# A hybrid attention block: transfers, normalising and weight splits at the begin of retention put in another order

## Chip, cores, metric

One core of one Trainium2 chip runs the whole program as one launch. The metric is the device time of that launch in microseconds, as the median of several runs.

## What is computed

The input X is 2 sequences of 2048 rows by 256 numbers. Two layers of retention and feed-forward (FFN) come first, then a ternary FFN, a window attention and a second ternary FFN. The change touches the begin of both retention layers and the FFN behind each. A layer of the reference, cut to what matters:

```python
for i in range(L):                                  # L = 2 layers, H = 8 heads of 32
    Xn = _layernorm(X, ln1_w[i], ln1_b[i])
    Q, K, V = Xn @ WQ[i], Xn @ WK[i], Xn @ WV[i]    # per head
    Q = Q * cosq + _rotate_every_two(Q) * sinq
    K = K * cosk + _rotate_every_two(K) * sink
    Yh = ((Q @ K.T) * decay_mask) @ V
    Y = _groupnorm(Yh, gn_w[i], gn_b[i])
    Y = (silu(Xn @ WG[i]) * Y) @ WO[i] + X
    Yn = _layernorm(Y, ln2_w[i], ln2_b[i])
    X = silu(Yn @ ffn_w1[i] + ffn_b1[i]) @ ffn_w2[i] + ffn_b2[i] + Y
```

The layers get the layernorm of the input, without weights (the kernel normalises its rows of X in place, and folds this into the first layer's scale, hence the factor 1 + EPS).

## The kernel before

**Tiling.** X stays in SBUF as 32 chunks of 128 rows (`X[:, 32, 256]`). Four chunks are a block (`TB`), and blocks alternate between the two sequences: block 0 is chunks 0 to 3, block 1 is chunks 16 to 19. Every product of fp32 numbers is made as three passes over split operands: a high half on ACT (`high_half`, L79, or the second activation of L1486) and a low half on DVE (`low_half`, L85, or L1277).

**The order of work.** Each engine has its own instruction stream, written out by hand; semaphores connect them. `retention` runs `body(i)` over steps of one chunk: a step is `k` of `U = 8`, and chunk `n = 8 i + k - 8` is projected in it, so that `i = 0` only prepares block 0 and chunk 0 starts at `i = 1, k = 0`. In the step of chunk n PE does, in this order: `project_heads(n)` (Q and K, L1645 into `pj`), `scores(n-1)` (L1712), `project_values(n)` (L1645 into `sc`), in even steps `gate_product` (L1645) and `transposes` of the next block's normalised rows (L1687), in odd steps from step 7 on `out_product` and `transpose_outputs`, then `transpose_heads(n)` (L1697), `chunk_out(n-1)` (L1725 to L1736) and `transpose_back(n-2)`. Between them lie: DVE `rotate` (L1288, L1291: reads `pj`), POOL `rotary_sum` (L1194), PE `transpose_heads`, ACT `heads_out` (L1493). `scores(n)` waits for `heads_out(n)`, for DVE's `values(n)` and for `in_done`, which DVE gives in `next_state(n-1)` (L1317).

**A block's rows** are made ready so: DVE `statistics` (L1263, one per chunk) and `aggregate` (L1271), POOL `scales` (five small operations, L1162 to L1177, the power at L1169 the longest), ACT `normalise` (L1462, four) into `xn`, PE `transposes` in two halves of columns (L1687) into the one bank `tr[1]`, ACT `inputs` (two activations per half, L1486), DVE `input_low` (L1277). ACT's `rows_in_place` (L1470) normalises X itself in layer 0.

**Transfers.** In layer 0, SyncE issues X block by block (L1137; it waits for `wqkv` before the second) and then, when all five low halves of the layer's own weights are done, the FFN's weights (L68). ACT issues, ahead of its first computation, `wqkv`, `ident`, `ln1`, `wg`, `wo` and ten tables: 15 issues (L68). It then loads its function table (L1631). DVE centres the value weights (`centre_values`, L1236 and L1239) ahead of the low halves `own_low(0..2)`, and does `own_low(3..4)` at `k = 4`; ACT's high halves match.

**FFN weights** are split during `i = 1`: one `high_half` on ACT and one `low_half` on DVE in each of the eight steps, at the end of a step.

**FFN, POOL.** `body` at L469 makes the scale of block g (L387, L389) and adds constants to the rows of block g - 1 (`add_constants`: L466, and in the second layer L461 ahead of it), in that order per g; at g = 2 it adds those of block 0 as well. DVE `normalise` (L539) of block 3 waits for scale 3, and PE's transposes (L876) for that.

## Time and profile before

| | |
|---|---|
| median of 3 runs | 1512.28 us (1511.6 to 1513.19) |
| the profiled execution | 1512.02 us, span 1510.2 us |
| mean granted clock of TensorE | 0.989 |
| PE / PEld busy | 1441.6 / 1195.5 us |
| DVE / ACT / POOL busy | 1032.2 / 936.4 / 830.2 us |
| PE by 40 slices, in tenths | 4999999999998999999999999998999999989997 |

The span runs from the first to the last instruction; what lies around it is 1.8 us. A slice is 37.8 us; a 9 is a busy share of 90% or more. In the timelines below a line gives start, length, engine, source line, operation, output and inputs, the count of merged instructions, and in brackets how long the engine had been idle and what ended it.

### The profile page before, as it was taken

What the parts mean: (1) busy time and instruction counts of PE and PEld (TensorE: products, weight loads), DVE (VectorE), ACT (ScalarE), POOL (GpSimd) and SP (SyncE); (2) the same over time, 40 slices, a digit from 0 to 9 for tenths busy, and PEclk for the clock granted to TensorE, in tenths of its full rate; (3) what the DMA queues carried; (4) which work ended last, traced back from release to release, by engine and by line L of the source; (5) the groups of instructions that cost most, each with busy time, mean ns of one, the idle gap of its engine ahead of it and who ended that gap; (6) DMA issues with size and microseconds to landing.
All of it is one profiled execution on the core that took longest, in us unless ns stands there. A gap on an engine that the chain in (4) does not pass through costs nothing. (4 is left out here: it accounts for less than half of the span.)

```text
span 1510.2 us, 36387 instructions
## 1 busy us (share of the span) xinstructions
PE 1441.6 (95%) x13066; PEld 1195.5 (79%) x13066; DVE 1032.2 (68%) x2272; ACT 936.4 (62%) x1760; POOL 830.2 (55%) x915
## 2 busy tenths in 40 slices
PE   4999999999998999999999999998999999989997
PEld 3777777899986788888899988886777777768886
DVE  4777877565546887785655678765777777756774
ACT  5555555565554545545655567775777777757775
POOL 2576676412103666663734357776666666636674
PEclk9999999999999999999999999999999999999999
DMA  7000000100001000000300010000000000000101
GB/s 248 2 2 2 0 2 2 36 1 1 1 1 56 2 2 0 1 2 2 124 29 15 1 40 2 0 1 1 2 1 0 0 0 0 0 2 2 40 31 43
DMA packets 21096, 26.27 MB, mean 17 GB/s; under 512 B 1905, under 2 KB 19057, under 8 KB 20849
## 3 DMA queue, kind: packets, MB, share of 16 engines
q1 hardware_dynamic: 18432, 21.64, 4.4%
q10 hardware_dynamic: 2544, 3.04, 0.6%
q8 instruction: 75, 1.23, 0.3%
q14 instruction: 45, 0.36, 0.1%
HBM read 20.48 MB, written 4.19 MB: 16 GB/s over the span
## 5 line engine op out<-in xcount | busy, mean ns | idle before, releaser
L546 DVE TENSOR_TENSOR ffn_h_lo<-ffn_h,ffn_h_hi 128x512 fp32r<-128x512 f32 x112 | 85.8, 766 | 121.6 <-ACT ffn_h_hi L753 121.6
L752 ACT ACTIVATE ffn_h<-ffn_hp,c_b 128x512 f32<-128x512 f32 x112 | 77.2, 689 | 146.3 <-PE ffn_hp L849 145.8
L546 DVE TENSOR_TENSOR ternary_ffn_h_lo<-ternary_ffn_h,ternary_ffn_h_hi 128x512 fp32r<-128x512 f32 x128 | 110.4, 862 | 77.4 <-ACT ternary_ffn_h_hi L753 77.1
L1194 POOL TENSOR_TENSOR ret_qk<-ret_qk,ret_qk_sin 128x512 f32<-128x512 f32 x64 | 82.6, 1290 | 103.5 <-DVE ret_qk_sin L1291 103.1
L860 PE MATMUL ternary_ffn_yp<-down_ternary,ternary_ffn_h_hi 128*128 128x256 f32 x512 | 132.3, 291 | 0.0
L860 PE MATMUL ffn_yp<-down_hi,ffn_h_hi 128*128 128x256 f32 x448 | 127.4, 284 | 0.0
L860 PE MATMUL ternary_ffn_yp<-down_ternary,ternary_ffn_h_lo 128*128 128x256 f32 x512 | 127.4, 280 | 0.0
L1200 POOL TENSOR_TENSOR ret_rstd<-ret_sums,ret_minus_half 128x16 f32<-128x16 f32 x32 | 103.7, 3239 | 42.9 <-DVE ret_sums L1333 42.9
L860 PE MATMUL ffn_yp<-down_hi,ffn_h_lo 128*128 128x256 f32 x448 | 125.0, 279 | 0.0
L860 PE MATMUL ffn_yp<-down_lo,ffn_h_hi 128*128 128x256 f32 x448 | 124.9, 279 | 0.0
L443 POOL TENSOR_TENSOR ternary_ffn_h_sq<-ternary_ffn_h_sq 128x512 f32<-128x512 f32 x61 | 95.0, 1566 | 42.4 <-ACT ternary_ffn_h_sq L759 38.7
L2089 POOL TENSOR_TENSOR win_rms<-win_rms,win_minus_half 128x20 f32<-128x20 f32 x31 | 115.0, 3710 | 2.6
L2313 ACT ACTIVATE wa_probs_t<-wa_tp 128x512 f32<-128x512 f32 x128 | 76.4, 597 | 63.5 <-PE wa_tp L2490 63.0
L752 ACT ACTIVATE ternary_ffn_h<-ternary_ffn_hp 128x512 f32<-128x512 f32 x128 | 76.4, 597 | 54.6 <-PE ternary_ffn_hp L849 48.0
L849 PE MATMUL ternary_ffn_hp<-xt_hi,up_ternary 128*128 128x512 f32 x256 | 103.3, 404 | 4.3 <-DVEq L729 4.3
L849 PE MATMUL ternary_ffn_hp<-xt_lo,up_ternary 128*128 128x512 f32 x256 | 102.6, 401 | 0.0
L860 PEld LDWEIGHTS ternary_ffn_yp<-down_ternary,ternary_ffn_h_hi 128*128 128x128 f32 x512 | 96.4, 188 | 7.1 <-issue 3.8
L860 PEld LDWEIGHTS ternary_ffn_yp<-down_ternary,ternary_ffn_h_lo 128*128 128x128 f32 x512 | 96.6, 189 | 3.2
L1288 DVE TENSOR_TENSOR ret_qk<-ret_pj,rotary 128x512 f32<-128x512 f32 x64 | 44.2, 691 | 71.9 <-PE ret_pj L1645 71.9
L849 PE MATMUL ffn_hp<-xt_hi,up_hi 128*128 128x512 f32 x224 | 88.9, 397 | 2.4 <-DVEq L729 2.4
L1301 DVE TENSOR_TENSOR ret_probs<-ret_sc,causal 128x1024 f32<-128x1024 f32 x64 | 78.4, 1224 | 16.2 <-issue 11.2
L849 PE MATMUL ffn_hp<-xt_lo,up_hi 128*128 128x512 f32 x224 | 88.8, 397 | 0.0
(315 smaller groups left out, 4724.3 us busy)
## 6 DMA issues: line engine op xcount, KB each, us to landing
X<-in_x SPq DMA_DIRECT2D x8, 512.0 KB, 10.1
staging<-in_w SPq DMA_DIRECT2D x4, 1024.0 KB, 8.5
ffn_x_in<-in_x SPq DMA_DIRECT2D x8, 512.0 KB, 3.8
out<-X SPq DMA_DIRECT2D x7, 512.0 KB, 2.9
rotary<-in_rotary ACTq DMA_DIRECT2D x1, 1024.0 KB, 7.5
staging<-in_w_up SPq DMA_DIRECT2D x1, 1024.0 KB, 4.9
staging<-in_w_down SPq DMA_DIRECT2D x1, 1024.0 KB, 7.5
staging<-in_wqkv ACTq DMA_DIRECT2D x1, 768.0 KB, 6.0
```

The source lines that it names most:

```text
L443: nc.gpsimd.tensor_tensor(h_sq[:, m, :], h_sq[:, m, :], h_sq[:, m + 1, :], ALU.add).then_inc(sq_added, 1)
L546: nc.vector.tensor_tensor(h_lo[:, m % R, :], h[:, m % R, :], h_hi[:, m % R, :].bitcast(F32), ALU.subtract).then_inc(h_ready, 1)
L752: nc.scalar.activation(h[:, m % R, :], hp[m % 2][:, :], fn, bias=bias)
L849: last = nc.tensor.matmul(hp[m % 2][:, :], w[:, j, m * P:(m + 1) * P], x[:, k, j, :], start=(n == 0), stop=(n == len(todo) - 1))
L860: last = nc.tensor.matmul(yp[k][t // 2][:, (t % 2) * D:(t % 2 + 1) * D], x[:, m % R, t * P:(t + 1) * P], w[:, m, :], start=(m == 0 and t % ...
L1194: nc.gpsimd.tensor_tensor(qk[:, r, :, :, :], qk[:, r, :, :, :], qk_sin[:, r, :, :, :], ALU.add).then_inc(qk_done, 1)
L1200: nc.gpsimd.tensor_tensor(rstd[:, :], sums[:, 1, :], minus_half[:, :], ALU.pow).then_inc(rstd_done, 1)
L1288: nc.vector.tensor_tensor(qk[:, r, :, :, :], src, cos, ALU.mult)
L1301: nc.vector.tensor_tensor(pr[:, at % 2, :, :, :], sc[:, :, 0:HT].rearrange("p h (j n) -> p h j n", j=NG), causal[:, :].unsqueeze(1).unsque ...
L2089: nc.gpsimd.tensor_tensor(rms[:, 1, :], rms[:, 0, :], minus_half[:, :], ALU.pow).then_inc(rms_work, 1)
L2313: nc.scalar.activation(pt[:, g, :, :].rearrange("p c n -> p (c n)"), tp[:, :], ACT.Copy).then_inc(pt_done, 1)
```

## The change

SyncE issues everything for layer 0 but `ident` and `ln1`: X's first block as four tiles with a semaphore each, `wqkv`, `wg`, `rotary` and `decay`, X's block 1, `wo` and the other tables, the other blocks of X. ACT issues two transfers, loads its function table from a constant that POOL sets, and waits for `ln1` only at its first `inputs`. The scale of blocks 0 and 1 is cut in two on POOL: `first_scale` (add, power), which alone is needed to normalise, and in layer 0 `scale_in_place` for X itself. DVE normalises blocks 0 and 1 (`first_normalise`). The second transposes of block 0 go to `tr[0]`, and `project_heads(0)` starts on the first half of the columns. Block 1's statistics move into chunk 0's step, its normalising and first transposes into chunk 1's; in both layers. `centre_values` moves behind the low halves of Q and K, the splits of values and gate behind `inputs`, that of `out_w` into chunk 0's step. The FFN weights' splits are made two at a time in the last four steps of `i = 1`. In the FFN, scale 3 is made ahead of `add_constants(1)`. The diff, cut to its core (`...` stands for context or for accounting of semaphores):

```diff
                         if begun and isinstance(g, int) and g == 2:      # ffn, POOL
                             add_constants(0, 0, 0)
+                            scales(3, 1)
...
+        def transposed(b, j):
+            return tr[0] if first is not None and at_start(b) and j == 1 else tr[1]
...
-                for b in range(NB):                                      # retention, SyncE
+                for t in range(TB):
+                    sp.dma_start(X[:, t, :], first["x"][P * t:P * (t + 1), :]).then_inc(tile_loaded[t], 16)
+                prefetch(sp, first["weights"][0:1], qkv_loaded)
+                prefetch(sp, first["weights"][1:2], gate_loaded)
+                prefetch(sp, first["tables"][0:2], rotary_loaded)
+                for b in range(1, NB):
                     at = b // 2 + CPB * (b % 2)
-                    if b == 1:
-                        sp.wait_ge(qkv_loaded, 16)
+                    if b == 2:
+                        prefetch(sp, first["weights"][2:], weights_loaded)
+                        prefetch(sp, first["tables"][2:], tables_loaded)
                     sp.dma_start(X[:, TB * at:TB * (at + 1), :],
...
+            def first_scale(b):                                          # POOL
+                pool.wait_ge(mv_done, b + 1)
+                apart(pool, pool_waited)
+                nc.gpsimd.tensor_scalar(work[:, 0, 0, :], mv[:, b, :, 1], ...).then_inc(eps_added, 1)
+                pool.wait_ge(eps_added, b + 1 if first is None else 2 * b + 1)
+                nc.gpsimd.tensor_tensor(scale[:, b, 0, 0, :], work[:, 0, 0, :], minus_half[:, 0:TB], ALU.pow
+                                        ).then_inc(first_scaled, 1)
+            def scale_in_place(b):    # add, power, product, negation for X itself: four operations
...
                     if k % TB == TB - 1 and fresh(2 * i + k // TB):
-                        scales(2 * i + k // TB, k // TB)
+                        if not at_start(i):
+                            scales(2 * i + k // TB, k // TB)
+                        elif k == TB - 1:
+                            first_scale(0)
+                            scale_in_place(0)
+                    if at_start(n):           # behind rotary_sum(0), ahead of rotary_sum(1)
+                        first_scale(1)
+                        if first is not None:
+                            scale_in_place(1)
...
+            def first_normalise(b):                                      # DVE
+                dve.wait_ge(first_scaled, b + 1)
+                if b == 1:
+                    dve.wait_ge(tp_full, KD)
+                for t in range(TB):
+                    last = nc.vector.tensor_scalar(xn[:, t, :], X[:, CPB * TB * b + t, :], mv[:, b, t, 0:1],
+                                                   scale[:, b, 0, 0, t:t + 1], ALU.subtract, ALU.mult)
+                last.then_inc(xn_done, 1)
...
                     if first is not None and at_start(n):
-                        dve.wait_ge(tables_loaded, 16 * len(first["tables"]))
+                        dve.wait_ge(rotary_loaded, 16 * 2)
...
                     if live(n, NT):
                         values(n, k)
+                    if at_start(n):
+                        for t in range(TB):
+                            statistics(1, 0, 1, t)
+                        aggregate(1, 1)
+                        if first is not None:
+                            own_low(4)
+                    if at_start(n - 1):
+                        first_normalise(1)
...
                         if fresh(2 * i + at):
                             input_low(2 * i + at, k % TB // 2, at)
+                        if first is not None and at_start(i) and k == U - 1:
+                            own_low(2)
+                            own_low(3)
...
                     if live(n - 1, NT):
                         next_state(n - 1, k - 1)
...
                     if at_start(i) and k == TB - 2:
                         if first is not None:
+                            first_normalise(0)
+                            for j in range(2):
+                                own_low(j)
                             centre_values()
-                            for j in range(3):
-                                own_low(j)
...
-                    if isinstance(i, int) and i == 1 and k < len(halves):
-                        dve.wait_ge(hi_done, k + 1)
-                        low_half(nc, halves[k])
+                    if isinstance(i, int) and i == 1 and k >= U // 2:
+                        for j in range(2 * k - U, 2 * k - U + 2):
+                            dve.wait_ge(hi_done, j + 1)
+                            low_half(nc, halves[j])
...
-                        if t == 0 and fresh(b + 1):                      # ACT
+                        if t == 0 and fresh(b + 1) and not at_start(b) and not at_start(b + 1):
                             normalise(b + 1, i, at + 1)
...
+                        if t == 2 and first is not None and at_start(b):
+                            act.wait_ge(scale_done, 2)
+                            rows_in_place(1, i, at + 1)
...
                     if live(n, NT):
                         heads_out(n, k)
+                    if at_start(n - 1):
+                        inputs(1, 0, 1)
...
+                    if first is not None and at_start(n):
+                        act.wait_ge(weights_loaded, 16 * (len(first["weights"]) - 2))
+                        own_high(4)
+                        act.wait_ge(tables_loaded, 16 * (len(first["tables"]) - 2))
...
-                prefetch(act, first["weights"][0:1], qkv_loaded)
                 prefetch(act, first["early"], early_loaded)
-                prefetch(act, first["weights"][1:], weights_loaded)
-                prefetch(act, first["tables"], tables_loaded)
-                act.wait_ge(early_loaded, 16 * len(first["early"]))
-                nc.scalar.activation(table_set[:, :], ident[:, 0:1], ACT.Silu)
+                act.wait_ge(consts_set, 1)
+                nc.scalar.activation(table_set[:, :], minus_half[:, 0:1], ACT.Silu)
...
-                    pe.wait_ge(xt_ready, KD * (b + 1))                   # PE, project_heads
+                    pe.wait_ge(xt_ready, 1 if halved else KD * (b + 1))
...
-                        if fresh(b + 1):
+                        if fresh(b + 1) and not at_start(n):
                             transposes(b + 1, t // 2, 4 * i + (k - AHEAD) // 2 + 2)
...
                         chunk_out(n - 1, k - AHEAD - 1)
+                    if at_start(n - 1):
+                        transposes(1, 0, 2)
```

## Rows read from the trace of the kernel before

**Rows 1.** The page, part 1

```profile
PE 1441.6 (95%) x13066; PEld 1195.5 (79%) x13066; DVE 1032.2 (68%) x2272; ACT 936.4 (62%) x1760; POOL 830.2 (55%) x915
```

**Rows 2.** Waits of PE over the whole run: total us, times, longest

```profile
PE ret_tr L1687 <- ACT xn L1462: 19.2, 8, 15.1
```

**Rows 3.** Timeline, first 22 us: start, us, engine, line, operation, [idle before]

```profile
7.24 1.41 DVE L1263 BATCH_NORM_STATS2 ret_stats<-X 128x6 f32<-128x256 f32 x4 [7.24 <-DMA X<-in_x]
...
8.79 0.38 DVE L1271 BATCH_NORM_AGGREGATE mean_var<-ret_stats 128x2 f32<-128x6 f32 x4
...
9.77 0.77 DVE L1239 SCALAR_TENSOR_TENSOR staging<-ret_v_weight_sums,staging 128x256 f32<-128x256 f32 x2
...
10.87 1.90 DVE L85 TENSOR_TENSOR qkv_lo<-staging,qkv_hi 128x512 fp32r<-128x512 f32 x3 [0.33 <-ACT qkv_hi L79]
...
12.91 2.07 ACT L1462 ACTIVATE xn<-X,ret_scale 128x256 f32<-128x256 f32 x4 [1.03 <-POOL ret_scale L1177]
...
15.13 1.09 PE L1687 MATMUL ret_tr<-c_ident,xn 128*128 128x128 f32 x4 [15.13 <-ACT xn L1462]
...
16.25 0.78 ACT L1486 ACTIVATE xt<-ret_tr,c_ln 128x512 f32<-128x512 f32 x1 [0.23 <-PE ret_tr L1687]
...
20.38 0.69 DVE L1277 TENSOR_TENSOR xt_lo<-xt,xt_hi 128x512 fp32r<-128x512 f32 x1 [0.45 <-ACT xt_hi L1486]
```

**Rows 4.** Windows (columns as part 1's engines, then granted clock, DMA share, GB/s)

```profile
12.00:15.00 3.00, 0.00 (x0) 0.00 (x0) 1.20 (x3) 2.09 (x5) 0.68 (x2) 1.00 1.17 319
...
32.40:39.10 6.70, 5.64 (x45) 4.24 (x46) 3.42 (x8) 1.50 (x3) 1.00 (x1) 0.50 0.01 2
```

**Rows 5.** Line L1137: SyncE's issues of X, ns min/median/max

```profile
L1137 SPq DMA_DIRECT2D X<-in_x x8: 387/1004/2057, 0.7 to 13.9; - x8
```

**Rows 6.** Timeline, first steps of layer 0

```profile
21.22 0.77 PE L1645 MATMUL ret_pj<-qkv_hi,xt_hi 128*128 128x512 f32 x1 [2.35 <-DVE xt_lo L1277]
...
25.67 1.29 POOL L1194 TENSOR_TENSOR ret_qk<-ret_qk,ret_qk_sin 128x512 f32<-128x512 f32 x1 [2.07 <-DVE ret_qk_sin L1291]
...
30.10 0.69 DVE L85 TENSOR_TENSOR up_lo<-staging,up_hi 128x512 fp32r<-128x512 f32 x1 [3.85 <-ACT up_hi L79]
...
33.45 1.11 PE L1697 MATMUL ret_tr<-c_ident,ret_qk 128*128 128x128 f32 x4 [2.72 <-POOL ret_qk L1194]
...
39.58 0.73 PE L1712 MATMUL ret_sc<-ret_qkt 32*128 32x128 f32 x16
```

**Rows 7.** Timeline, begin of layer 1's retention

```profile
454.09 0.50 PE L1645 MATMUL ret_pj<-qkv_hi,xt_hi 128*128 128x512 f32 x1 [2.40 <-DVEq L1451]
...
457.60 1.04 POOL L1169 TENSOR_TENSOR ret_scale<-ret_scale_work,ret_minus_half 128x4 f32<-128x4 f32 x1
...
461.53 0.66 PE L1687 MATMUL ret_tr<-c_ident,xn 128*128 128x128 f32 x4 [2.13 <-ACT xn L1462]
...
471.74 0.73 PE L1712 MATMUL ret_sc<-ret_qkt 32*128 32x128 f32 x16
```

**Rows 8.** Timeline, the two feed-forward stages behind the retentions

```profile
291.78 6.63 POOL L466 TENSOR_TENSOR X<-X,c_b 128x256 f32<-128x256 f32 x8
...
292.23 3.04 DVE L539 TENSOR_SCALAR xn<-X,mean_var,scale 128x256 f32<-128x256 f32 x4
...
721.27 1.38 DVE L539 TENSOR_SCALAR xn<-X,mean_var,scale 128x256 f32<-128x256 f32 x4
...
740.96 3.01 DVE L539 TENSOR_SCALAR xn<-X,mean_var,scale 128x256 f32<-128x256 f32 x4 [2.64 <-POOL scale L389]
...
744.02 0.66 PE L876 MATMUL ffn_tp<-c_ident,xn 128*128 128x128 f32 x4 [2.58 <-DVE xn L539]
```

**Rows 9.** Timeline, step 7 of layer 0

```profile
74.33 0.69 DVE L1288 TENSOR_TENSOR ret_qk<-ret_pj,rotary 128x512 f32<-128x512 f32 x1
...
74.94 0.75 DVE L1291 TENSOR_TENSOR ret_qk_sin<-ret_pj,rotary 128x256 f32<-128x256 f32 x2
...
77.55 0.60 PE L1697 MATMUL ret_tr<-c_ident,ret_qk 128*128 128x128 f32 x4
```

More of the change, by code:

```diff
@@ L473, in body @@
                     if not ternary:
-                        if unmeasured(g):
+                        if unmeasured(g) and not first_after_begun(g):
                             scales(g, k)
@@ L1068, in retention @@
         x_loaded = [sem(f"x_loaded{k}") for k in range(NB)] if first is not None else []
+        tile_loaded = [sem(f"tile_loaded{t}") for t in range(TB)] if first is not None else []
+        rotary_loaded, first_scaled, gate_loaded = sem("rotary_loaded"), sem("first_scaled"), sem("gate_loaded")
         x_done = sem("x_done")
@@ L1260, in statistics @@
                     at_least(dve, mv_done, b)
-                    if first is not None and not last_block(b) and not after_last(b):
-                        x_wait(b, at)
+                if first is not None and not last_block(b) and not after_last(b) and (t == 0 or at_start(b)):
+                    x_wait(b, at, t)
                 nc.vector.bn_stats(stats[:, t, :], rows(i, at, t).rearrange("p o d -> p (o d)")
@@ L1406, in body @@
                     if first is not None and at_start(n):
-                        dve.wait_ge(tables_loaded, 16 * len(first["tables"]))
+                        dve.wait_ge(rotary_loaded, 16 * 2)
                     if live(n, NT):
                         rotate(n, i, k - AHEAD)
+                    if first is not None and at_start(n - 1):
+                        dve.wait_ge(tables_loaded, 16 * (len(first["tables"]) - 2))
                     if live(n - 1, NT):
@@ L1429, in body @@
                         next_state(n - 1, k - 1)
[L1430 removed]
+                    if at_start(i) and k >= TB:
+                        pass
+                    elif fresh(2 * i + k // TB) or (after_last(2 * i + k // TB) and i == N):
                         if k % TB < TB - 1:
@@ L1603, in body @@
                     else:
-                        if fresh(b + 1):
+                        if first is not None and at_start(i) and k == TB + 1:
+                            act.wait_ge(early_loaded, 16 * len(first["early"]))
+                        if fresh(b + 1) and not at_start(n - 1):
                             inputs(b + 1, t // 2, at + 1)
+                        if first is not None and at_start(i) and k == U - 1:
+                            act.wait_ge(v_centred, 1)
+                            own_high(2)
+                            act.wait_ge(gate_loaded, 16)
+                            own_high(3)
                         half = (k - AHEAD - 5) // 2
@@ L1639, in _, with three @@
             xs = (xt_hi, xt_lo)
-            def three(out, x, w):
+            def three(out, x, w, second=None):
                 todo = [(j, a, c_) for j in range(KD) for a, c_ in ((0, 0), (0, 1), (1, 0))]
                 for m, (j, a, c_) in enumerate(todo):
+                    if second is not None and m == len(todo) // KD:
+                        pe.wait_ge(xt_ready, second)
                     last = nc.tensor.matmul(out, x(a, j), w(c_, j), start=(m == 0), stop=(m == len(todo) - 1))
@@ L1654, in project_heads @@
                     pe.wait_ge(own_lo_done, 2)
+                halved = at_start(n) and first is not None
                 if at % TB == 0:
-                    pe.wait_ge(xt_ready, KD * (b + 1))
+                    pe.wait_ge(xt_ready, 1 if halved else KD * (b + 1))
                 at_least(pe, qk_read, n)
-                three(pj[0][:, :], tokens(at), lambda a, j: qkv[a][:, j, 0:2 * D]).then_inc(qk_full, 1)
+                three(pj[0][:, :], tokens(at), lambda a, j: qkv[a][:, j, 0:2 * D], KD if halved else None
+                      ).then_inc(qk_full, 1)
             def project_values(n, at):
@@ L1683, in transposes @@
                     pe.wait_ge(yt_read, m - 4)
-                else:
+                elif not (first is not None and at_start(b)):
                     at_least(pe, xt_read, m)
                 for t in range(TB):
-                    last = nc.tensor.transpose(tr[1][:, t * P:(t + 1) * P], xn[:, t, j * P:(j + 1) * P],
+                    last = nc.tensor.transpose(transposed(b, j)[:, t * P:(t + 1) * P], xn[:, t, j * P:(j + 1) * P],
                                                ident[:, :])
@@ L1763, in out_product @@
                 pe.wait_ge(gy_ready, q + 1)
+                if at_start(q) and first is not None:
+                    pe.wait_ge(own_lo_done, 5)
                 if live(q + 3, 2 * NB):
```

53 lines of the change are left out of this document (31 added, 22 removed).

## The prediction, made before the changed kernel had run

> **What bounds the kernel now.** The page comes first: PE is busy 95% of the span and every other engine less than 70% [rows 1], so a microsecond counts only where PE stands still or runs at a lower clock. The waits of PE say where: 19.2 us on ACT's normalised rows, 15.1 of them at the very begin [rows 2]. I then read the begin as a timeline. X's first block is there at 7.24, DVE measures it until about 9.2, five POOL operations and four ACT operations follow, PE's first transposes stand at 15.13, and project_heads(0) starts at 21.22 [rows 3, 6]. Behind that, rotate(1) sits behind a weight split (DVE idle 3.85 for it), PE idles 2.72 for POOL's sum, and from 32.4 to 39.1 the granted clock is 0.50, that is 1.2 GHz, after PE's pause ahead of 33.45 [rows 4, 6]. scores(1) at 39.58 is my first marker: from there the steps are PE's own work. Layer 1 has the same shape, smaller: start 454.09, a wait of 2.13 for ACT's rows, scores(1) at 471.74 [rows 7]. The second FFN has a wait of PE of 2.58, behind DVE, which waited 2.64 for POOL's scale [rows 8]. So 21.2 + 18.4 us, 17.65 us and 2.6 us are what the change can touch.
>
> **Layer 0, up to project_heads(0).** It removes: the whole block as one transfer, four of the five POOL operations, ACT's normalising, and the wait of the second transposes for tr[1]. Transfers: the earliest block came at 7.24 while wqkv shared the engines. Alone at 319 GB/s or more [rows 4], 512 KB take 1.6 us less 0.4 for the last tile's neighbours; issues cost 0.39 us at least [rows 5]. I put the last tile at 5.0 (between 4.4 and 5.9). wqkv now stands behind X on one queue, but both had landed by 9.8, when DVE used them, and the bytes ahead of it are no more than then, so it is there before DVE is free for it at 9.0. Then: one tile's statistics, 1.41/4 = 0.4, gives 5.4; aggregate with its gap 0.5, so 5.9; add and power on POOL with two hand-overs, 0.6 + 1.04 [rows 7], 7.6; first_normalise(0) 1.38 [rows 8], 9.0; transposes 1.1, 10.1; two activations 1.5, 11.6. DVE meanwhile does own_low(0..1), 2 x 0.63 = 1.3, and centre_values, reduce and two operations, about 1.45 from the 0.77 of the two [rows 3], so it is free at 11.75; input_low 0.69, 12.45. With a hand-over PE starts at 12.6 instead of 21.22: **8.6 us earlier** (bounds 6.4 and 9.3). The second half of the columns is ready at 13.8, under the first three passes. rotary is 2.7 MB down the queue, at 319 GB/s there by 11.8; rotate(0) wants it at about 15.6. values and gate are split by 15.1, in time. ACT's table load disappears beside the transfers: nothing, and 1.3 us are there to cover it.
>
> **Layer 0, to scores(1).** values(0) and gate(0) end at about 18.3 if PE's first 4 us (my assumption) go at the pace of its first pass, 0.77 [rows 6], heads(0) 18.5 to 19.0, project(1) until 20.5. DVE now has block 1's statistics (1.41 + 0.5) behind values(0), so mv stands at 19.25. What is queued behind it matters: POOL does first_scale(1), 0.6 + 1.04 + 0.3, and then scale_in_place(1), four operations, some 2.7 us, *ahead of* rotary_sum(1), 1.29 [rows 6]. That sum ends at about 24.8, though rotate(1) is over at 22.8 (itself 0.9 late behind own_low(4) and block 2's first statistics). PE stands for 2.2 us at heads(1), about what it stands now. Then heads(1) and chunk_out(0), 2.1, give 26.9, the moved transposes 0.6, 27.5. Here the change adds a wait that was not there: DVE's input_low(1, 0) stands ahead of next_state(0), and scores(1) waits for in_done. Transposes 27.5, ACT's two activations 29.0, input_low 29.7, state 30.0: scores(1) at 30.0 instead of 28.6. rotate(2), behind them, is late by 0.4 more. 30.4 - 12.6 = 17.8 against 18.4: **0.6 us less**. The old stretch at 1.2 GHz (6.7 us, PE busy 5.64) goes with its cause, but a pause of 2.2 us ahead of a step is of the size that brought it; I charge 1.2 us for a stretch of half that length. **Net -0.6 + 1.2 = +0.6**; bounds -2.5 (no low clock, no 2.2 us pause in full) and +3.
>
> **Layer 1.** Block 1's statistics no longer stand ahead of rotate(0), and PE's 2.13 us wait and its 0.5 us of transposes leave step 0: heads(0) at 459.4. project(1) 1.5, scores and values 1.5, POOL's sum in step with rotate(1) (there is no scale in place here, and the power ends at 460.9), heads(1) at 464.3; 2.05 and 0.6 bring 466.9; the new chain ACT, input_low, state takes 2.5: 469.4, and rotate(2) 0.35. 469.75 against 471.74: **-2.0 us** (bounds 0 and -3.2, the latter without the chain).
>
> **FFN.** In the first one scale 3 waits for DVE either way; 0. In the second the scale moves ahead of add_constants(1), which occupied POOL for some 7 us (eight such operations take 6.63 in the first FFN): DVE's 2.64 go. DVE's four operations still run beside POOL's additions, 3.0 us, from 738.3 to 741.3, and PE wants them at 741.45: **-2.4 us** of 2.58 (bounds 1.6 and 2.6).
>
> **Weight splits, two per step.** The first four steps lose 0.68 us of DVE each, which PE's waits hide. In step 7 rotate starts at 74.33 without any idle time ahead of it [rows 9]: the extra 0.66 and about 0.2 inherited from step 6 push it by 0.86. Its two operations and POOL's sum need 0.69 + 0.75 + 1.29, ending at 77.05, and PE takes it at 77.55: 0.5 us of cover, so **+0.4 us per layer**, +0.8 (bounds 0 and 1.7). Without that cover it would be 0.86 in each.
>
> **Sum.** -8.6 + 0.6 - 2.0 - 2.4 + 0.8 = -11.6. From the profiled 1512.0 this gives 1500.4; the median shown is 0.3 higher, so I write **1500.5**.
>
> **A rule against this change.** DVE's four normalising operations take 1.38 us with POOL idle and 3.04 beside POOL's additions, which began first [rows 8]. In the new order first_normalise(0) runs beside scale_in_place(0), and first_normalise(1) beside rotary_sum(1). My sum takes 1.38, since the nearer POOL operations have 4 numbers per partition and not 256. The Trainium skill (SBUF — State Buffer, section Who interferes with whom) says that such a DVE operation and a GpSimd operation lock a shared port pair, and that the second to issue is blocked for the whole of the first. By that rule the trace agrees for the large additions, and a power of 1 us would hold DVE as well; it would make the sum 1503.7, as rival 1, where the rows as I read them give 1500.5.
>
> **Rivals.**
> 1. *DVE and POOL block each other.* Price 3.04 - 1.38 = 1.66 in full ahead of project_heads(0), and 1.66 less some 0.8 of cover in front of the moved transposes, in each layer: +3.3, **1503.7**. For it: the rows just named. Against it: small operations. 0.18.
> 2. *PE stays at 2.4 GHz and the tiles come early.* -2.5 instead of +0.6 in layer 0's steps, and 0.6 from the transfer: **1497**. 0.12.
> 3. *The doubled splits become the bound.* DVE has no idle time ahead of rotate(7) now; if every one of the four steps pays 0.66 in both layers, +5.3 - 0.8: **1505**. Against it: two of the four steps have a rotation that waits for PE. 0.04.
> 4. *The new order hides nothing*, because wqkv, now behind X on one queue, lands as late as it is early now: if own_low waits until 20, project_heads(0) starts as before and only 3 us of the rest are left: **1509**, within or next to no change. Against it: the bytes ahead of it are the same as before. 0.03.
> 5. *Slower.* DVE's statistics of block 2 stand in chunk 0's step, ahead of rotate(1), and wait for that block's transfer, now SyncE's 19th issue and 4.5 MB down one queue. At 319 GB/s it is there at about 18, and rotate(1) wants DVE at 21.4. Issues took up to 2.06 us under load [rows 5]; nineteen such, 39 us, would hold every engine for 18 us: **1518**. It decides from a landing at 33 us on. Against it: a median of 1.0, and the queue's total is unchanged. 0.02.
>
> **How the numbers follow.** The forecast has 0.61, the rivals 0.18, 0.12, 0.04, 0.03 and 0.02. The range 1496.5 to 1505 takes in the forecast's bounds as far as they are independent (their squares' sum is about 4 us), and rivals 1 to 3. 0.2% is 3.0 us, about what a measurement of this kernel can tell: faster 0.95, same 0.03, slower 0.02.
>
> **What would show it.** Right: project_heads(0) at 12 to 13.5; first_normalise(0) near 1.4; scores(1) 17 to 19 us later; PE idle some 2 us at heads(1) in layer 0, for POOL; in both layers a short PE wait ahead of scores(1), for DVE's state; scores(1) of layer 1 15.5 us after its start instead of 17.65; no wait of DVE for the FFN's scale; PE's transposes of step 7 released by POOL. Wrong: first_normalise at 3 us (rival 1), a wait of DVE for X in chunk 0's step (5), of ACT for wqkv beyond 9 us (4), or a granted clock of 0.5 over more than one stretch behind project_heads(1).

## The result, and the profile after

The changed kernel takes 1498.1 us in the median of 4 runs (1496.82 to 1500.4), the kernel before 1512.7 (1511.6 to 1513.19, 4 runs): a ratio of 0.9909, 95% interval 0.9898 to 0.9921, 14.6 us less where 11.8 were forecast. The profiled execution took 1497.22 us, 14.8 less than the profiled one of before.

The page of the changed kernel, parts 1 and 2. PE's busy time is 10.4 us less [rows 1] though its instructions are about the same in number: stretches at half the clock have gone, and not only waits.

```profile
PE 1431.2 (96%) x13034; PEld 1188.7 (79%) x13066; DVE 1035.8 (69%) x2284; ACT 929.8 (62%) x1748; POOL 831.9 (56%) x915
...
PEclk9999999999999999999999999999999999999999
```

Waits of PE over the run (total us, times, longest). The 19.2 us for ACT's rows [rows 2] are 9.9 for DVE's, once, and 3.0 for ACT's; the last row, 2.2 us for DVE's state (1.08 in each layer), is new.

```profile
PE ret_tr L1773 <- DVE xn L1406: 9.9, 1, 9.9
PE ret_tr L1783 <- POOL ret_qk L1233: 8.4, 8, 2.1
...
PE ret_tr L1773 <- ACT xn L1536: 3.0, 7, 1.2
...
PE ret_sc L1798 <- DVE ret_state_in L1366: 2.2, 2, 1.1
```

The begin as a timeline (start, us, engine, line, operation, idle before), the counterpart of [rows 3]. The tiles are there one by one, POOL does two operations ahead of DVE's rows and not five, and project_heads(0) starts at 13.53, not 21.22 [rows 6]. DVE's rows take 1.39 though POOL's power runs beside them (8.77 to 9.83).

```profile
5.49 0.77 DVE L1312 BATCH_NORM_STATS2 ret_stats<-X 128x6 f32<-128x256 f32 x2 [1.49 <-DMA X<-in_x]
...
7.33 1.04 POOL L1201 TENSOR_TENSOR ret_scale<-ret_scale_work,ret_minus_half 128x4 f32<-128x4 f32 x1
8.41 1.39 DVE L1406 TENSOR_SCALAR xn<-X,mean_var,ret_scale 128x256 f32<-128x256 f32 x4 [1.62 <-POOL ret_scale L1201]
...
8.77 1.06 POOL L1209 TENSOR_TENSOR ret_scale<-ret_scale_work,ret_minus_half 128x4 f32<-128x4 f32 x1
9.30 1.15 ACT L79 ACTIVATE qkv_hi<-staging 128x512 fp32r<-128x512 f32 x2 [6.13 <-DMA staging<-in_wqkv]
...
12.69 0.69 DVE L1326 TENSOR_TENSOR xt_lo<-xt,xt_hi 128x512 fp32r<-128x512 f32 x1
...
13.53 0.77 PE L1729 MATMUL ret_pj<-qkv_hi,xt_hi 128*128 128x512 f32 x1 [1.65 <-DVE xt_lo L1326]
```

The first steps of layer 0 and the begin of layer 1, timelines of the same execution. heads(1) waits 2.11 for POOL in layer 0; in layer 1, scores(1) waits 1.08 for the state, which stands behind ACT's two activations and input_low. Compare [rows 6, 7].

```profile
25.05 0.66 PE L1783 MATMUL ret_tr<-c_ident,ret_qk 128*128 128x128 f32 x4 [2.11 <-POOL ret_qk L1233]
...
458.50 0.77 ACT L1560 ACTIVATE xt_hi<-ret_tr,c_ln 128x512 fp32r<-128x512 f32 x1
...
459.30 0.69 DVE L1326 TENSOR_TENSOR xt_lo<-xt,xt_hi 128x512 fp32r<-128x512 f32 x1 [2.51 <-ACT xt_hi L1560]
459.91 0.22 DVE L1366 TENSOR_TENSOR ret_state_in<-ret_sc,ret_own_state 128x64 f32<-128x64 f32 x1
...
460.27 0.73 PE L1798 MATMUL ret_sc<-ret_qkt 32*128 32x128 f32 x16 [1.08 <-DVE ret_state_in L1366]
```

Where the 14.9 us of the span come from, by the starts of PE's work in the two profiles:

| | before | after | gained |
|---|---|---|---|
| project_heads(0) | 21.22 | 13.53 | 7.7 |
| from there to scores(1) | 18.36 | 16.73 | 1.6 |
| scores(1) to scores(8) | 49.77 | 50.60 | -0.8 |
| layer 1, start to scores(1) | 17.65 | 14.62 | 3.0 |
| scores(1) to scores(8) | 49.18 | 49.96 | -0.8 |
| second FFN | 168.97 | 166.24 | 2.7 |
| window attention and second ternary FFN, which the change doesn't touch | 475.7 | 474.2 | 1.5 |

The rows agree with the stages to 0.1. The last one is chance: over the twelve other executions profiled in this case the window attention alone took 323.8 to 326.4 us, and in the two profiles compared here these last stages hold four stretches of 3.4 us at a granted clock of 0.5 before, two after, ahead of the one at the very end that both have.

### The profile page after: what moved, and what is told of

Same layout as the page of the kernel before. It is cut to its first block and busy times, and to the rows that moved or that the text cites. A ratio compares the mean times of both kernels' runs of the same rounds, so it can differ in the third digit from the quotient of the medians.

```text
span 1495.3 us, 36363 instructions
## 1 busy us (share of the span) xinstructions
PE 1431.2 (96%) x13034; PEld 1188.7 (79%) x13066; DVE 1035.8 (69%) x2284; ACT 929.8 (62%) x1748; POOL 831.9 (56%) x915
## 3 DMA queue, kind: packets, MB, share of 16 engines
q8 instruction: 75, 1.23, 0.3%
```

## The experiments

Each is an edit of the changed kernel, shown shortened; where a range follows the time it is that of 4 runs. They are judged by starts of PE's instructions, which repeat better than the total: scores(1) to scores(8) in layer 0 was 50.58 to 50.61 in the seven executions that have the changed kernel's steps 1 to 7. The start of layer 1 is that of its project_heads(0); expectations that speak of layer 1's first transposes mean the same point.

**1. The transfers as before.**

```
-  SyncE: X by tiles, wqkv, wg, rotary, X block 1, wo and tables, X ...
+  SyncE: X block 0 in one, wait for wqkv, X blocks 1 to 7
+  ScalarE: wqkv, identity and norm, wg, wo, tables
```

> Undo only the transfers: ScalarE issues wqkv first, then identity, norm, wg, wo and tables; SyncE issues X's first block as one transfer and the rest behind wqkv. Theory (the early tiles are a term of their own): DVE's last first-block statistics end at about 8.7 instead of 5.8, project_heads(0) starts 2.3 to 2.9 us later than 13.53, at 15.8 to 16.4, and the whole is longer by 2.3 to 2.9 us. Rival (wqkv's landing sets the pace, since ScalarE's first weight half waited for it until 9.3 in the changed kernel): wqkv lands earlier here, the chain on it is shorter, and project_heads(0) moves by less than 1 us.

1500.84 us (1498.7 to 1503.13). The first statistics stand at 7.21, where the kernel before had them [rows 3], and project_heads(0) at 15.88:

```profile
7.21 1.41 DVE L1304 BATCH_NORM_STATS2 ret_stats<-X 128x6 f32<-128x256 f32 x4 [7.21 <-DMA X<-in_x]
...
15.88 0.77 PE L1726 MATMUL ret_pj<-qkv_hi,xt_hi 128*128 128x512 f32 x1 [1.64 <-DVE xt_lo L1318]
```

So the transfers' order is worth 2.35 us against the profile, and 3.1 against the median of the begin (below). The edit moves wqkv as well as the tiles, but the tiles alone set the start: from the end of DVE's last first-block statistics (8.61 here, 6.26 in the changed kernel's profile) to project_heads(0) it is 7.26 or 7.27 us in all twelve executions with this chain, wherever between 7.23 and 10.23 ACT began to split wqkv. The rival falls.

**2. Layer 0's first block normalised on ACT, with the whole scale.**

```
-  POOL: first_scale(0), scale_in_place(0);  DVE: first_normalise(0)
+  POOL: scales(0, 0) (both kinds);          ACT: own_high(0..1), normalise(0)
```

> Undo only the way in which layer 0's first block is normalised: the five-operation scale on POOL and four activations on ACT, behind ACT's two weight halves, as before. Theory (a term of its own): POOL's last scale operation ends about 1.9 us after first_scale's power, so at about 10.3, ACT's four rows take about 1.6, the rows are done at about 12, against 9.8, and project_heads(0) starts at about 15.7, 2.2 us later than 13.53. Rival (DVE's own chain of weight halves and value centring sets the start of project_heads(0), since input_low stood behind it): DVE has 1.4 us less to do, and project_heads(0) moves by less than 1 us.

1502.16 us (1500.68 to 1503.37). project_heads(0) at 16.10, 2.57 later (3.4 against the median). Counted from the last statistics, which takes the transfers' spread out, it is 10.11 instead of 7.27, so this part is worth 2.84. DVE's weight splits and value centring were over at 11.14 here and PE still had no rows until 12.51, so they are not what sets the start:

```profile
10.29 2.07 ACT L1536 ACTIVATE xn<-X,ret_scale 128x256 f32<-128x256 f32 x4 [1.36 <-POOL ret_scale L1191]
10.38 0.76 DVE L1287 SCALAR_TENSOR_TENSOR staging<-ret_v_weight_sums,staging 128x256 f32<-128x256 f32 x2
...
12.51 1.94 PE L1774 MATMUL ret_tr<-c_ident,xn 128*128 128x128 f32 x8 [12.51 <-ACT xn L1536]
```

Of the 7.7 us at project_heads(0) in the table, 2.4 are the earlier statistics (8.64 before, 6.26 after) and 5.3 the shorter chain behind them (12.58 before, 7.27 after). Experiment 2 explains 2.84 of the 5.3; the rest (the second half of the columns under the first passes, tr[0], the order on DVE) was not taken apart.

**3. Layer 1's begin as before.**

```
-  moved for both layers: at_start(n)
+  moved for layer 0 alone: first is not None and at_start(n)
```

> Undo only layer 1's begin: block 1's statistics in the steps behind project(0), its five-operation scale, ACT's rows and PE's transposes in step 0, as before. Theory (the removed wait and the two DVE blocks ahead of rotate(0) are worth 2 us): layer 1's scores(1) comes 17.0 to 17.7 us after its first transposes instead of 14.62, its scores(8) 2 to 2.3 us later, and the whole is 2 to 3 us longer. Rival (luck of the granted clock: the kernel before had stretches at 0.5 in layer 1 and the changed one has none): without such a stretch the old order costs less than 1 us.

1501.04 us (1499.18 to 1502.03). Layer 1's scores(1) comes 17.60 us after its start, not 14.62, scores(8) 2.77 later, and the whole is 2.9 to 3.9 longer by the medians of the two sets of the changed kernel. PE's wait for ACT's rows is back, at 3.7 us (2.13 in [rows 7]). The rival spoke of an execution without a low stretch, and this was none: the granted clock is 0.75 over six us. The old begin brought the pause and the low stretch in both executions that have it; they were not told apart, and their sum is the price. The eleven profiles that have the moved begin in layer 1, and no weight split in its first three steps, show no such stretch behind heads(1), so its absence there is not the luck of one execution. First the wait (total, times, longest), then the window (busy time of PE, PEld, DVE, ACT, POOL, granted clock, DMA share, GB/s):

```profile
PE ret_tr L1776 <- ACT xn L1539: 6.7, 8, 3.7
```

The window behind that wait:

```profile
456.00:462.00 6.00, 5.17 (x48) 3.56 (x48) 3.13 (x6) 2.05 (x4) 1.27 (x1) 0.75 0.00 0
```

**4. The FFN's scale behind add_constants.**

```
-  if unmeasured(g) and not first_after_begun(g): scales(g, k)
-  scales(3, 1)                 (it stood behind add_constants(0, 0, 0), which stays)
+  if unmeasured(g): scales(g, k)
```

> Undo only the order of scale 3 and add_constants in the FFNs. Theory: PE's wait of 2.6 us behind DVE's normalising, and DVE's of 2.6 for POOL's scale, are back in the second FFN and only there: from its first PE instruction to that of the first ternary FFN it takes 168.9 us instead of 166.2, the first FFN's 166.9 stays within 0.2, and the whole is 2.6 us longer. Rival (the gain was the clock's): the wait is back, and the second FFN's length changes by less than 1 us.

1502.53 us (1500.74 to 1502.67). DVE waits 2.65 us again, PE's wait for xn is 2.6, the second FFN takes 169.00 and not 166.24, the first stays (166.92, 166.91):

```profile
731.68 1.04 POOL L389 TENSOR_TENSOR scale<-ffn_scale_work,ffn_powers 128x4 f32<-128x4 f32 x1
...
732.75 3.01 DVE L539 TENSOR_SCALAR xn<-X,mean_var,scale 128x256 f32<-128x256 f32 x4 [2.65 <-POOL scale L389]
```

So this part is worth 2.76 us: the stage took 166.2 in all twelve profiled executions that have it, and 169.0 in the two that don't. The whole is 4.4 to 5.3 us longer by the medians, more than the 2.6 expected. In the profiled execution much of the excess lies where the edit doesn't reach: the granted clock is low for 6.8 us in layer 0 (24.4 to 31.2), and layer 1's project(0) has a stretch too, so that its scores(1) comes 15.55 after the start and not 14.61:

```profile
447.60:451.00 3.40, 3.40 (x13) 2.94 (x12) 1.08 (x3) 0.00 (x0) 0.65 (x2) 0.51 0.82 254
```

**5. One weight split per step, as before.**

```
-  if ... i == 1 and k >= U // 2:  for j in (2 * k - U, 2 * k - U + 1)
+  if ... i == 1:                  for j in (k,)
```

> Undo only the spacing of the FFN's weight splits: one in each of the steps 0 to 7, as before, with all else as in the changed kernel. Theory (two splits in step 7 cost 0.4 to 0.6 us in each layer): scores(8) stands 49.8 to 50.0 us behind scores(1) in layer 0 instead of 50.60, and 49.2 to 49.4 in layer 1 instead of 49.96, as it did in the kernel before. Against it, DVE's 0.68 us of split 0 and of split 1 stand ahead of rotate(1) and rotate(2), so that scores(1) comes 0.3 to 0.7 us later in layer 1. Rival (the loss in step 7 belongs to the moved begin, not to the splits): both distances stay at 50.6 and 50.0.

One run, 1510.9 us, beside 1511.43 of the kernel before: nearly the whole gain is gone. This was in neither theory, which had scores(1) of layer 1 later by 0.7 at most: it is 3.9 later, and in layer 0 project_heads(0) to scores(1) takes 28.14 instead of 16.73. The splits did give back what was expected, scores(2) to scores(8) falls from 43.30 to 42.70 in layer 0 and from 42.67 to 42.10 in layer 1; but split 0 in step 0 waits for the FFN's weights, whose transfer starts when out_w is split, and DVE's rotate(1) is behind it:

```profile
21.10 0.89 SPq L68 DMA_DIRECT2D staging<-in_w  x2
...
29.76 0.63 ACT L79 ACTIVATE up_hi<-staging 128x512 fp32r<-128x512 f32 x1 [9.41 <-DMA staging<-in_w]
30.42 0.69 DVE L85 TENSOR_TENSOR up_lo<-staging,up_hi 128x512 fp32r<-128x512 f32 x1 [9.01 <-ACT up_hi L79]
...
33.78 0.47 PE L1783 MATMUL ret_tr<-c_ident,ret_qk 128*128 128x128 f32 x1 [11.61 <-POOL ret_qk L1233]
```

It costs layer 1 as well: ACT's half waits for the landing there, 7.79 us after the start, and rotate(1) follows the low half without a pause.

```profile
463.83 0.63 ACT L79 ACTIVATE up_hi<-staging 128x512 fp32r<-128x512 f32 x1 [1.35 <-DMA staging<-in_w]
```

In the kernel before DVE waited for the same split, where I had not looked: a new row of its trace,

```profile
463.90 0.69 DVE L85 TENSOR_TENSOR up_lo<-staging,up_hi 128x512 fp32r<-128x512 f32 x1 [4.91 <-ACT up_hi L79]
```

But there it was not the landing that ended last. ACT began its half at 463.25, right behind heads_out(0), which had waited for PE and so for the rows; and rotate(1) then waited 0.72 us more, for PE. The landing was hidden, and it shows only once the rows are early. With experiment 3 the four corners are there. Start to scores(1) of layer 1, us:

| | one split per step | two in steps 4 to 7 |
|---|---|---|
| begin as before | 17.65 (before) | 17.60 (exp. 3) |
| begin moved | 18.52 (exp. 5) | 14.62 (changed) |

Each edit alone gives nothing, or less than nothing; only together do they give 3 us. Two late inputs lay over each other, the weights' landing and PE's wait for ACT's rows, and either one holds the step. The prices hold the clock's part too, which was not told apart: a corner is one profiled execution, and all but the changed kernel's have a stretch of 3.4 us at a granted clock of 0.5 behind the pause (pauses of 2.13, 3.67 and 3.09 us; behind 1.23 in the changed kernel there is none).

**6 and 7. Where the doubled splits hurt.** Eight splits over steps 3 to 7, first as 2, 2, 2, 1, 1, then as 2, 2, 1, 1, 2:

```
+  if i == 1:  for j in {3: (0, 1), 4: (2, 3), 5: (4, 5), 6: (6,), 7: (7,)}.get(k, ())
+  if i == 1:  for j in {3: (0, 1), 4: (2, 3), 5: (4,), 6: (5,), 7: (6, 7)}.get(k, ())
```

> The eight weight splits as two, two, two, one and one over steps 3 to 7, instead of two in each of 4 to 7. Theory A (ACT's second high half in step 7 holds up the yt chain that ends in step 8's rows) and theory B (DVE's two low halves of step 6, ahead of rotate(7), hold up POOL's sum and with it the same chain) both expect the loss to go: scores(8) 0.5 to 0.6 us less behind scores(1) in both layers, 50.0 and 49.4, and PE's wait for ACT's rows at step 8 back at 0.7 from 1.23. If it stays at 50.6 neither is right, and what is lost comes from step 5 or from the begin.

> The same eight splits as two, two, one, one and two over steps 3 to 7. Theory A (ACT in step 7): the loss stays, scores(8) 50.5 to 50.6 us behind scores(1) in layer 0. Theory B (DVE's low halves ahead of rotate(7), of which only one is left here): the loss goes, 50.0 us, as with the other spacing.

One run each, 1497.39 and 1495.65. scores(2) to scores(8), us, in layers 0 and 1: changed 43.30, 42.67; first spacing 42.70, 42.09; second 42.91, 42.08. With two splits still in step 7, 1.0 of 1.2 us are back: ACT's doubled work there is not the cause, theory B holds but for 0.2 in layer 0. The rows put that 0.2 down to POOL: its last scale operation of step 7 runs beside the second of DVE's two low halves and takes 0.46 us, in all three executions with this spacing, and 0.25 in all others, and PE's wait at step 8 is 0.94 instead of 0.74:

```profile
69.84 1.30 DVE L85 TENSOR_TENSOR down_lo<-staging,down_hi 128x512 fp32r<-128x512 f32 x2 [0.38 <-ACT down_hi L79]
...
70.79 0.46 POOL L1191 TENSOR_SCALAR ret_scale<-ret_scale_work 128x8 f32<-128x8 f32 x1 [0.20 <-POOL ret_scale_work L1186]
```

The chain in the changed kernel is: two low halves on DVE from 64.55 to 65.81, rotate(7) and POOL's sum behind them, POOL's scale and gate behind that, and ACT's gated rows ahead of the normalising that PE wants in step 8. Its last links:

```profile
72.47 1.28 POOL L1248 TENSOR_TENSOR ret_yt<-ret_yt,ret_gate 128x512 f32<-128x512 f32 x1
...
73.86 0.63 ACT L1604 ACTIVATE ret_gy_hi<-ret_yt 128x512 fp32r<-128x512 f32 x1 [1.46 <-POOL ret_yt L1248]
...
76.59 0.65 PE L1773 MATMUL ret_tr<-c_ident,xn 128*128 128x128 f32 x4 [1.23 <-ACT xn L1536]
```

and with the first spacing (scores(1) is 0.99 later there) the wait is shorter by the half microsecond:

```profile
76.98 0.65 PE L1773 MATMUL ret_tr<-c_ident,xn 128*128 128x128 f32 x4 [0.74 <-ACT xn L1536]
```

**8. The state ahead of the low half.**

```
 DVE, chunk 1's step
+  next_state(0)
   input_low(1, 0)
-  next_state(0)
```

> One change to the changed kernel: in chunk 1's step DVE does next_state(0) ahead of input_low(1, 0), not behind it, in both layers. Theory (the change made scores(1) wait for ACT and input_low, 1.08 us of PE's time in each layer): the wait for ret_state_in goes, and layer 1's scores(1) comes 13.5 to 13.7 us after its first transposes instead of 14.62; rotate(2) stays where it is, so that scores(2) gains about 0.7 less 0.0 to 0.4. The whole: 0.6 to 1.4 us less. Rival (the chain through rotate(2) and its POOL sum bounds the step anyway): scores(1) is earlier, scores(2) is not, by less than 0.2 us.

One run, 1494.42. scores(1) of layer 1 comes 14.12 after the start, not 13.5 to 13.7; scores(2) 21.20, from 21.91: 0.71 gained, as the theory had for the whole step, and 0.72 in layer 0. The total, 2.8 to 3.7 below the changed kernel's medians, is one execution without a stretch at the low clock in layer 0, and no measure of the edit. The other half microsecond turned into a wait for ACT, whose columns_out(0) stands behind its two activations:

```profile
458.13 0.73 PE L1799 MATMUL ret_sc<-ret_qkt 32*128 32x128 f32 x16 [0.62 <-ACT ret_y_cols L1579]
```

**9. POOL's sum ahead of its second scale, and out_w's split behind the rows.**

```
 POOL                         DVE, layer 0
   first_scale(1)             -  own_low(4)      (chunk 0's step)
-  scale_in_place(1)             rotate(1) ... first_normalise(1)
   rotary_sum(1)              +  own_low(4)
+  scale_in_place(1)
```

> Two moves in layer 0, chunk 1's step: POOL does rotary_sum(1) ahead of scale_in_place(1), and DVE does own_low(4) behind first_normalise(1), not ahead of rotate(1). Theory (PE's pause of 2.1 us at heads(1) is POOL's queue and DVE's, and this pause is what brings the stretch at a granted clock of 0.5 in some executions and not in others): the pause shrinks to 1.1 to 1.4 us, scores(1) comes 19.3 to 19.7 us after PE's first transposes, against 20.3 in an execution without such a stretch and 22.1 in one with it, and no low stretch follows. The whole: 0.7 us less than an undisturbed execution, 1 to 1.5 less in the median. Rival (the low stretch does not hang on this pause): the pause shrinks, the granted clock still falls in the profiled execution, and scores(1) comes 21.3 us after the first transposes.

1495.67 us (1495.09 to 1497.22), 1.5 less than the changed kernel beside it by the medians, with ranges that overlap. The pause is 1.23 and not 2.11, scores(1) comes 19.44 after the first transposes, 0.88 earlier than in the undisturbed profile, and the granted clock stays at 1.00. The two moves were not taken apart. The timeline also has DVE's four rows beginning 0.04 us behind a power on POOL, and taking 1.37 all the same:

```profile
23.33 0.66 PE L1783 MATMUL ret_tr<-c_ident,ret_qk 128*128 128x128 f32 x4 [1.23 <-POOL ret_qk L1233]
...
23.68 1.12 POOL L1209 TENSOR_TENSOR ret_scale<-ret_scale_work,ret_minus_half 128x4 f32<-128x4 f32 x1
23.72 1.37 DVE L1406 TENSOR_SCALAR xn<-X,mean_var,ret_scale 128x256 f32<-128x256 f32 x4
```

**10. The changed kernel again.**

> The changed kernel again, unaltered, for the spread that its begin has from one execution to the next and as the measure for the combination. Theory: PE's first transposes between 9.0 and 10.0 us, scores(1) either about 20.3 us or about 22.1 us after them, according to whether a stretch at 0.5 follows heads(1), scores(8) 50.6 behind scores(1); the median 1497 to 1500. Rival (the difference between 20.3 and 22.1 belongs to the edits and not to chance): 20.3 again, as in the first profile.

1497.19 us (1495.57 to 1498.36). The rival falls: the same kernel, and now the clock is low behind heads(1), as the windows show (columns as in experiment 3), and scores(1) comes 21.91 after the first transposes, not 20.32.

```profile
25.10:27.90 2.80, 2.80 (x41) 2.05 (x40) 0.83 (x3) 0.60 (x1) 0.00 (x0) 0.60 1.04 376
27.90:29.00 1.10, 1.10 (x5) 1.00 (x4) 0.00 (x0) 0.45 (x1) 0.00 (x0) 0.50 0.95 297
```

Over all profiles with the pause of some 2 us at heads(1), 6 of 9 have this stretch (the changed kernel again, experiments 1 to 4 and 6); of the three with a pause of 1.23 (experiments 9, 11, 12) none has. That speaks for the pause as a condition; three executions don't prove it. The other stretches of layer 1's begin fit: heads(1) there waits some 1.23 us in eleven executions, and none has a low stretch behind it. A pause is not enough, though. Ahead of layer 1's project_heads(0) PE stands 2.40 to 2.46 us in all fourteen profiles, and the clock falls behind it in three (before, experiments 4 and 5).

**11. All that helped, together.** Experiments 7, 8 and 9, with own_low(4) behind next_state(0), and on ACT

```
+  columns_out(0)
   inputs(1, 0)
-  columns_out(0)     (was at the head of the next step)
```

> All that helped, together: DVE does next_state(0) ahead of input_low(1, 0), ACT does columns_out(0) ahead of inputs(1, 0) (PE waited 0.6 us for it once the state came first), POOL's rotary_sum(1) ahead of scale_in_place(1), own_low(4) behind next_state(0), and the weight splits as two, two, one, one, two over steps 3 to 7. Theory (the gains add, less 0.1 to 0.3 where two meet on rotate(2)): from the changed kernel -0.7 in each layer for the state and the columns, -0.6 and -0.4 for the splits, -0.9 for POOL's order, so 3.0 to 3.5 us less than the changed kernel in the same call, near 1494 to 1495. Rival (they shorten the same wait): 1.5 us or less.

1493.81 us (1492.69 to 1495.2), ratio to the kernel before 0.9884 (0.9868 to 0.9901); 3.4 us less than the changed kernel beside it, as expected, and with ranges that don't meet. scores(1) has no wait in layer 1, but heads(2) has a new one of 0.42 for POOL's sum, and scores(2) comes 21.16 after the start, hardly earlier than in experiment 8: the gains of the state and of the columns meet on rotate(2).

```profile
460.81 0.66 PE L1785 MATMUL ret_tr<-c_ident,ret_qk 128*128 128x128 f32 x4 [0.42 <-POOL ret_qk L1233]
```

**12. The low half behind rotate(2).**

```
 DVE
-  input_low(1, 0)     (chunk 1's step)
   rotate(2)
+  input_low(1, 0)
```

> The combination with one move more: DVE does input_low(1, 0) behind rotate(2), not ahead of it. Theory (with the state first, rotate(2) is what sets chunk 2's step: PE waited 0.42 us for its POOL sum in layer 1): rotate(2) comes 0.3 to 0.6 us earlier, the wait of 0.42 goes in each layer, and scores(2) comes 20.7 to 20.8 us behind layer 1's first transposes instead of 21.16, 25.8 in layer 0 instead of 26.22; the whole 0.8 us less than the combination, a ratio to the kernel before of 0.988. Rival (another wait stands right behind, for ACT's qkt or for DVE's masked probabilities): scores(2) gains less than 0.15.

1493.79 us (1493.27 to 1494.29), ratio 0.9878 (0.9862 to 0.9895). scores(2) comes 20.54 after layer 1's start (0.62 less) and 25.90 after layer 0's first transposes (0.32 less); the rival falls. By the medians it can't be told from experiment 11: its profiled window attention took 326.2 us against 324.3. Both beat the changed kernel.

## Why the prediction was right, and where it was off

1500.5 was forecast; 1498.1 lies in the range of 1496.5 to 1505, 2.4 us from the value. The mechanisms stand where they were named; several sizes were off, and part of the nearness is that they were off in both directions.

**project_heads(0) at 12.6.** 13.53 in the first profile, which turned out the latest of eleven executions with this begin: 12.59 to 13.53, median 12.74. The tiles' landing makes the spread: PE's first transposes stand at 9.01 to 9.94, and behind the statistics all is the same to 0.01 (experiment 1). wqkv is there for ACT between 7.23 and 9.30. The single steps were right within 0.5, the last tile among them (5.0 assumed; statistics over at 6.3 in the profile, 5.8 in experiments 3 and 4).

**To scores(1): a stretch at the low clock, at 1.2 us.** As forecast: it comes after the 2.2 us pause, which is there with its cause as named (POOL's second scale ahead of the sum). It comes in six of the nine executions. From project_heads(0) to scores(1) it is 16.7 us in the two executions of these steps without it (first profile, experiment 7) and 18.3 to 18.7 in the four with it (3, 4, 6, 10), where before had 18.36. So the forecast +0.6 is -1.6 in the one case and 0 to +0.35 in the other, and the stretch costs 1.6 to 2.0, not 1.2. Without the stretch the sum had 17.8, and 16.73 was measured. Two terms were too large: POOL's second scale, put at 2.7 us, took 2.1 (21.64 to 23.76), and the 0.4 for a late rotate(2) falls behind scores(1) and is 0.2 there (7.30 from scores(1) to scores(2), 7.09 before). Rival 2 (1497, the clock stays high) was thus chance in the first profile, and not a rival of the mechanism: the clock stayed high, but its early tiles did not come.

**The added wait for the state.** Foreseen in its place, and measured at 1.08 in layer 1. Undone it gives 0.7 per layer.

**Layer 1, -2.0: it was -3.0.** The step that failed is "heads(0) at 459.4", 5.3 us after the start: 4.56 was measured. The rest of the difference is the 0.35 for rotate(2), which again falls behind scores(1). I took the old stage's own pace for its first microseconds, and they had run at 1.2 GHz; a row of before that I had not weighed there:

```profile
455.60:459.00 3.40, 3.40 (x12) 2.93 (x11) 3.25 (x12) 0.00 (x0) 1.47 (x3) 0.50 0.93 367
```

The new order is not free of this stretch either. In experiment 4 it came, heads(0) stood at 5.49 and scores(1) at 15.55, near the 15.5 forecast; in the ten other executions with the moved begin and the moved splits it did not come. And the attribution failed, not only the size. The prediction put layer 1's whole gain down to the moved block and priced the moved splits as a cost of 0.4. The corners of experiments 3 and 5 show that the two are one gain. DVE's wait of 4.91 for the split was in the trace, and the transfer behind it; I had looked for its like in layer 0 [rows 6] only.

**The FFN, -2.4: 2.73, and 2.76 undone.** The bound of 2.6 was the PE wait itself; with the scale moved DVE is so early that the whole of it goes, and 0.15 to 0.18 more, which no run explains. 0 in the first FFN was right.

**Doubled splits, +0.4 per layer: 0.60 and 0.57** from scores(2) to scores(8). The step that failed is the place. It said that PE takes heads(7) with 0.5 us of cover; between scores(6) and scores(7) only 0.11 are lost. The rest comes one step later, through POOL's queue and ACT's, at the normalised rows. The cover of the next instruction was counted, not that of the chain behind it.

**Rival 1 (DVE and POOL block each other) is refuted** by the 1.39 at 8.41, and by the 1.37 of experiment 9, which begins behind a running power. Beside POOL's sum first_normalise(1) hardly stood: that was over at 455.0 in layer 1, and DVE began at 455.4. By the rule (the Trainium skill, SBUF — State Buffer, section Who interferes with whom: of a DVE instruction in a two-port mode and a GpSimd one, the one that issues first holds the shared ports for its whole length) DVE would have waited until 24.80 in experiment 9 and ended near 26; it ended at 25.09, so the measurement decides against it for a power. No row shows which mode these four ran in; beside POOL's large additions the same form took 3.01 (experiment 4), so it does meet POOL there. Rival 4: wqkv came at 9.30 at the latest, not 20. Rival 5: no wait of DVE for block 2; own_low(4) ends at 21.85 and the statistics of block 2 start at 21.77 without any idle time.

The two larger misses have one sign, and the doubled splits (with the 0.2 of rotate(2) in each layer) the other: -2.2 to scores(1), -1.0 in layer 1, -0.3 in the FFN, -1.5 of chance in untouched stages, +0.9 at project_heads(0), +0.8 behind scores(1) make -3.3, the distance of the profiled 1497.2 from 1500.5.

## What to carry to other kernels

Where a step has two late inputs, undoing either edit alone shows the price of both: before calling one part useful or useless, look in the old trace for a second wait in the same step, and run both corners. When work is doubled up in a step, follow it past the next instruction, through the queues of the engines that share it, to the next wait of the bound engine. And a duration read in a stretch of low granted clock is no duration for the new order: read it again where the clock is full.

## What the runs showed of the hardware

The same kernel has the low clock behind the same pause in one execution and not in the next. With it goes how long the start ran slow. Of the nine executions with a pause of some 2 us at heads(1), the three without the low stretch are the three whose matmuls came to full pace soonest, 6.9 to 7.6 us behind the first transposes (8.0 to 9.7 in the other six). Experiments 11 and 12 came to full pace late, at 9.2 and 9.7, and with a pause of 1.23 had no stretch; experiment 9 did so at 7.6, so its own profile might have had none even with the longer pause. The first profile and experiment 10 are the two cases: in the first profile PE's 512-column matmuls start 0.43 us apart (1.2 GHz, though the column of the granted clock shows 1.00) until 17.5 and 0.23 behind it, in experiment 10 until 18.8, so that heads(0) waits for POOL in the one and not in the other. The start of PE's work and the end of the slow pace are not tied to each other. The Trainium skill (TensorE: Matmul & The Clock Gate, Part 1) says that the point of the rise varies from run to run of one kernel, and the runs agree.

Their start-to-start times, first in the first profile:

```profile
17.50 0.40 PE L1729 MATMUL ret_pj<-xt_hi,gate_hi 128*128 128x512 f32 x1
17.73 0.39 PE L1729 MATMUL ret_pj<-xt_lo,gate_hi 128*128 128x512 f32 x1
```

and in experiment 10, the same product, still 0.43 apart:

```profile
17.52 0.63 PE L1729 MATMUL ret_pj<-xt_hi,gate_lo 128*128 128x512 f32 x1
17.95 0.63 PE L1729 MATMUL ret_pj<-xt_hi,gate_hi 128*128 128x512 f32 x1
```

Where DVE and POOL did meet, POOL paid. Its multiplication of 128x4 numbers took 0.20 us when it began ahead of DVE's weight split (9.92 against 9.96) and 1.15 when it began behind it; in experiment 4:

```profile
9.25 1.28 DVE L85 TENSOR_TENSOR qkv_lo<-staging,qkv_hi 128x512 fp32r<-128x512 f32 x2
9.45 1.15 POOL L1211 TENSOR_TENSOR ret_scale_work<-mean_var,ret_scale 128x4 f32<-128x4 f32 x1
```

POOL's next work behind this chain came only at 17, so it cost PE nothing. In step 7 the like did cost PE: the 0.46 instead of 0.25 us of experiment 7 matches the 0.2 us that the second spacing leaves behind.
